# Two gated 3x3 convolutions on one core: the last image's second convolution in four blocks of 7, 7, 7 and 6 slots instead of three of 9, and short first-convolution blocks for one pair of images instead of two

## The reference

```
def qconv_cg(x, w, theta):                 # base = 64 // 4 = 16 channels
    yp = conv3x3(x[:, :base], w[:, :base])
    yr = conv3x3(x[:, base:], w[:, base:])
    d = sigmoid(2.0 * (yp - theta))
    return yp + d * yr

h   = relu(bn(qconv_cg(x, w_a, theta_a)))  # bn: a scale and a shift per channel
h   = bn(qconv_cg(h, w_b, theta_b))
out = relu(x + h)
```

## Time and profile before

| | before |
|---|---|
| median of 3 runs | 434.52 us (434.52 to 435.0) |
| the profiled execution's own time | 434.99 us |
| its span, first to last instruction | 433.1 us |
| time around the span | 1.89 us |
| TensorE (PE) busy | 426.2 us, 98% |
| VectorE (DVE) busy | 246.1 us, 57% |
| ScalarE (ACT) busy | 198.7 us, 46% |
| GpSimd (POOL) busy | 30.8 us, 7% |
| granted TensorE clock, mean | 0.996 |

### The profile page before, as it was taken

One profiled execution on the slowest core, in us unless ns is written; L12 is line 12 of the kernel. 1 busy time (PEld: TensorE's weight loads), 2 busy tenths in 40 slices (PEclk: granted clock), 3 DMA queues, 4 the chain that ended last, 5 costly groups with the idle time before them and its releaser, 6 DMA issues.

```text
span 433.1 us, 17330 instructions
## 1 busy us (share of the span) xinstructions
PE 426.2 (98%) x7823; PEld 423.9 (98%) x7823; DVE 246.1 (57%) x423; ACT 198.7 (46%) x338; POOL 30.8 (7%) x81
## 2 busy tenths in 40 slices
PE   9999999999999999999999999999999999999994
PEld 8999999999999999999999999999999999999993
DVE  6767644753764663574375385366357367436535
ACT  5765444534544553453453453354345355434322
POOL 6041000000000100000000000021000000000001
PEclk9999999999999999999999999999999999999998
DMA  8435116251615110420624161161623321012044
GB/s 166 87 79 98 27 27 123 50 98 29 122 28 101 25 28 4 99 51 2 125 57 82 37 123 29 27 123 25 122 49 62 66 49 39 13 27 49 8 93 94
DMA packets 119802, 27.57 MB, mean 64 GB/s; under 512 B 119408, under 2 KB 119664, under 8 KB 119728
## 3 DMA queue, kind: packets, MB, share of 16 engines
q1 hardware_dynamic: 117760, 26.09, 29.7%
q10 hardware_dynamic: 1648, 0.36, 0.4%
q0 software_dynamic: 320, 0.00, 0.0%
HBM read 13.60 MB, written 12.85 MB: 61 GB/s over the span
## 4 chain that ended last, share of the span: by engine, by line
PE 98%; DVE 1%; issue 0%; ACT 0%; DVEq 0%
PE acc L549 96%; PE acc L500 1%; DVE mix L863 0%; DVE rows_out L911 0%; PE acc L575 0%; PE acc L488 0%; ACT mix L697 0%; PE acc L492 0%; DVE rows_out L953 0%; DVE rows_out L908 0%; ACT rows_out L719 0%; DVEq L862 0%
## 5 line engine op out<-in xcount | busy, mean ns | idle before, releaser
L549 PE MATMUL acc<-x_lo,w_hi 32*128 32x456 f32 (+1 forms) x1392 | 251.3, 358 | 0.0
L549 PE MATMUL acc<-x_hi,w_lo 32*128 32x456 f32 (+1 forms) x1392 | 250.8, 358 | 0.0
L549 PE MATMUL acc<-x_hi,w_hi 32*128 32x456 f32 (+1 forms) x1392 | 250.5, 357 | 0.0
L549 PE MATMUL acc<-h_hi,w_lo 32*128 32x512 f32 x1152 | 244.2, 390 | 0.0
L549 PE MATMUL acc<-h_lo,w_hi 32*128 32x512 f32 x1152 | 243.7, 389 | 0.0
L549 PE MATMUL acc<-h_hi,w_hi 32*128 32x512 f32 x1152 | 243.5, 389 | 0.0
L549 PEld LDWEIGHTS acc<-x_lo,w_hi 32*128 32x128 f32 x1392 | 212.0, 183 | 0.0
L549 PEld LDWEIGHTS acc<-x_hi,w_lo 32*128 32x128 f32 x1392 | 211.8, 183 | 0.1
L549 PEld LDWEIGHTS acc<-x_hi,w_hi 32*128 32x128 f32 x1392 | 211.7, 183 | 0.0
L549 PEld LDWEIGHTS acc<-h_hi,w_hi 32*128 32x128 f32 x1152 | 183.9, 183 | 0.1
L549 PEld LDWEIGHTS acc<-h_hi,w_lo 32*128 32x128 f32 x1152 | 183.4, 183 | 0.0
(11 more groups left out here) (86 smaller groups left out, 161.3 us busy)
## 6 DMA issues: line engine op xcount, KB each, us to landing
out_dram<-rows_out SPq DMA_DIRECT2D x95, 126.0 KB, 2.5
x<-in_x_dram SPq DMA_DIRECT2D x28, 392.0 KB, 5.3
early<-in_x_dram SPq DMA_DIRECT2D x4, 112.0 KB, 3.7
x<-in_x_dram SPq DMA_DIRECT2D x4, 98.0 KB, 3.2
out_dram<-rows_out SPq DMA_DIRECT2D x3, 112.0 KB, 2.4
x<-in_x_dram SPq DMA_DIRECT2D x1, 294.0 KB, 4.3
x<-in_x_dram SPq DMA_DIRECT2D x1, 280.0 KB, 5.0
x<-in_x_dram SPq DMA_DIRECT2D x1, 196.0 KB, 3.5
```

What stands on the lines that cost most here:

```text
L549: return pe.matmul(sums(bank, blk), w[g * ROWS:(g + 1) * ROWS, tap], moving(blk, part, c, dx, g), start=(u == 0 and (alone or g == bank_gr ...
```

## The change

1. `SHORT_PAIRS` goes from 2 to 1: images 2 and 3 are cut like the later ones, into seven blocks of 8 slots instead of eight of 7. There are 57 a blocks.
2. The last image (15) has four b blocks, of 7, 7, 7 and 6 slots (`LAST`), instead of three of 9. They are b45 to b48, and there are 49 b blocks. Six slots are 342 columns.
3. The end of `second` becomes b45, b46, b44, b47, b48, e1 (before: b45, b46, b44, b47, e1).
4. The total stays 108 blocks and 27 rounds, and so does the number of matmuls, 108 x 4 x 18 = 7776.

The order that follows from lines 90 to 97, with the slots of each block, where the two differ most:

| round | before | after |
|---|---|---|
| r0, r1 | a0 to a7, all 7 | the same |
| r2 | a8:7 b0:9 a9:7 b1:9 | a8:8 b0:9 a9:8 b1:9 |
| r3 to r5 | the same pattern, 7 9 7 9 | the same pattern, 8 9 8 9 |
| r6 | a16:8 b8:9 a17:8 b9:9 | a16:8 a17:8 a18:8 a19:8 |
| r7 | a18:8 b10:9 a19:8 b11:9 | b8:9 a20:8 b9:9 a21:8 |
| r8 | a20:8 a21:8 b12:9 a22:8 | b10:9 a22:8 b11:9 a23:8 |
| r9 | b13:9 a23:8 a24:8 a25:8 | b12:9 a24:8 b13:9 a25:8 |
| r24 | b39:9 a56:8 b40:9 a57:8 | a55:8 b40:9 a56:8 b41:9 |
| r25 | b41:9 b42:9 b43:9 b45:9 | b42:9 b43:9 b45:7 b46:7 |
| r26 | b46:9 b44:9 b47:9 e1:8 | b44:9 b47:7 b48:6 e1:8 |

```
-SHORT, SHORT_PAIRS = 7, 2
+SHORT, SHORT_PAIRS = 7, 1
+LAST = (7, 7, 7, 6)
...
-    NB, NE = 3 * B, B // EDGE
+    NE = B // EDGE
...
-        second += [("b", 3 * img + r) for r in range(3)]
+        second += [("b", 3 * img + r) for r in range(3 if img < B - 1 else len(LAST))]
...
-    second[-4:] = [second[-3], second[-2], second[-4], second[-1], ("e", 1)]
+    second[-5:] = second[-4:-2] + [second[-5], second[-2], second[-1], ("e", 1)]

     def b_slots(n):

+        r = n - 3 * (B - 1)
+        if r >= 0:
+            return B - 1, 1 + sum(LAST[:r]), LAST[r]
         return n // 3, 1 + n % 3 * BLK_B, BLK_B
...
-        return BLK_B if kind == "b" else EDGE if kind == "e" else sum(k for img, t, k in a_slots[n])
+        return b_slots(n)[2] if kind == "b" else EDGE if kind == "e" else sum(k for img, t, k in a_slots[n])
```

## The result

The changed kernel takes 436.33 us (median of 8 runs, 435.91 to 438.21) against 434.83 us before (8 runs beside it): 1.0037 times as long, interval 1.0024 to 1.0049. It is slower by about 1.5 us, where 2.25 us were forecast. The profiled execution took 436.14 us, with a span of 434.3 us.

What follows compares the result with a forecast made beforehand. PE, busy 98% of the span with the row groups' matmuls, was taken as the bound. +4.2, -2.15, -0.1 and +0.3 give +2.25 us, 437.2 us from the profile; set on the 434.52 median, 436.8 us, range 435.4 to 438.2.

Steps and rivals of the forecast that it cites:

- Part 1: Everything up to the end of r24: 520 more columns at 8.1 ns each, +4.2 us.
- Part 2: r25 and r26: 512 fewer columns save only 2.15 us instead of 4.2, since nines delay one another.
- the path of nines: r25 and r26: visits through g2, g3, g1, g2, g3 meet nines in all but two pieces; short blocks wait beside it.
- a lead of two matmuls: PE's queue: a row group runs ahead by two matmuls, forgiving 0.46 us at each change of group.
- The sign that I had named: r25 and r26: matmuls of 398 and 342 columns 0.23 us apart beside nines; b44's product at about 425.5 us.
- Part 3: The tail after b44's last visit: chain unchanged, DVE's queue no longer late, 0.1 us less at most; last stores same sizes.
- Part 4: Load of image 7, split a round earlier: PE waits about 0.45 us, +0.3 us in sum, bounds 0 to +1.3.
- Free streams: r25 and r26: no limit on the lead acts there, PE's end moves +0.07 us; 434.6 to 434.9 us, chance 0.10.
- A lead of three: Row groups lead by three matmuls or more: +1.1 to +1.6 us instead of +2.05, 435.7 to 436.4 us; chance 0.17.
- Image 7 late: Image 7's load lands near the slowest 6.8 us or late gates push more: +1 to +1.3 us, 437.5 to 438.1; chance 0.13.

Runs made afterwards that it cites:

- shorts_less2: Changed kernel with two slots of each of the four short blocks b45 to b48 left out (5, 5, 5, 4); 436.2 us.
- b44_less2: Changed kernel with two slots of b44 alone left out (7 instead of 9); 434.32 us.
- cut_777: Kernel before with the last image's three b blocks cut to 7, 7, 7, six slots left out; 432.14 us.
- alternate: Changed kernel with the last image cut 7, 7, 6, 7 and long and short blocks in turn, b44 in r26; 435.6 us, 1.0018 times before.
- img7_late: Changed kernel with the load of image 7 issued behind b9's stores instead of b8's; 440.39 us.

## Why the prediction was right, and where its sizes were off

The direction, the mechanism and the order of the terms held; 1.5 us came instead of 2.25. That the time itself came nearer, 436.33 us against 436.8, is in part luck: the forecast was set on 434.52 us, the median of the first three of the 8 runs of the kernel before, and all 8 give 434.83.

**Part 1 (+4.2 us).** r1 to r24 took 4.05 us more in the first pair of profiles and 4.42 in the second, image 7's 0.1 to 0.2 us included. A small gain may be missing in the term: in the kernel before, where sevens are held in r2, r2 took 15.07 - 14.88 = 0.19 us more than r3 (0.09 in the second profile), and with eights beside nines r2 is no longer than r3. Two profiles of one kernel differ by 0.13 and 0.24 us in r1 to r24, so this is not shown.

**Part 2 (-2.15 us).** Measured -2.27 and -2.29, 0.1 us more than the term. Of all readings in the prediction this one decided the sign: by columns alone it would have been -4.2 and the change a draw. shorts_less2 and b44_less2 show that the path of nines sets the end, and cut_777 (2.0 to 2.2 us saved) and alternate (1.4) fit a lead of two matmuls. That the chip counts exactly two is not shown; it is the whole number that fits these kernels best. The sign that I had named came in part (timeline of the changed kernel, PE, r26): beside b44's nine the six's matmuls are 414.57 - 414.34 = 0.23 us apart and a seven's 415.06 - 414.83 = 0.23, but later, beside the nine in g3, the six's are only 423.83 - 423.67 = 0.16 apart. So the short blocks are not held all the time.

```profile
414.34 0.39 PE L553 MATMUL acc<-h_hi,w_lo 32*128 32x342 f32 x1
414.57 0.39 PE L553 MATMUL acc<-h_hi,w_lo 32*128 32x342 f32 x1
414.83 0.39 PE L553 MATMUL acc<-h_lo,w_hi 32*128 32x398 f32 x1
415.06 0.39 PE L553 MATMUL acc<-h_lo,w_hi 32*128 32x398 f32 x1
...
423.67 0.31 PE L553 MATMUL acc<-h_hi,w_hi 32*128 32x342 f32 x1
423.83 0.32 PE L553 MATMUL acc<-h_hi,w_hi 32*128 32x342 f32 x1
```

**Part 3 (-0.1 us at e1's sum).** b44's product came 1.79 us later than before and the last DVE instruction 430.92 - 429.19 = 1.73 us later: -0.06. POOL's addition ended last, as worked out. The step that failed is its last sentence, that the last stores have the same sizes. e1's store has, but the two blocks ahead of it in the DMA queue are seven and six instead of nine and nine, and the span ends 0.5 us sooner after the last instruction. This is the largest error of a single term.

**Part 4 (+0.3 us).** The place, the wait of some 4 us on ACT and the shift of b10's with_input came as described; the load landed 137.03 - 129.39 = 7.6 us after b8's relu instead of 8.4, so only 0.1 to 0.2 us reached PE, by r8 (15.90 and 16.03 us against 15.82 without the wait). img7_late shows that the cover was used up: a later landing goes straight into the time.

Sum of what the profiles show, first pair: +4.05 in r1 to r24, -2.27 in r25 and r26, -0.04 from the last matmul's start to DVE's end, -0.46 behind it, and -0.02 at the start, gives +1.26 us for the span (434.33 - 433.07). Second pair: +4.42 - 2.29 - 0.04 - 0.49, and +0.31 at the start, gives +1.91 us. Without the start, which does not go with the kernel, the two pairs give +1.28 and +1.60 us. The medians differ by +1.50 us.

**Rivals.** Free streams fell with shorts_less2. A lead of three was given 435.7 to 436.4 us, and the measured 436.33 lies in that too; the time alone does not tell it from the forecast. The two last rounds do: by the prediction's own sum three matmuls save 0.3 + 2.8 = 3.1 us there and two save 2.15, and 2.27 and 2.29 were measured. cut_777 too fits three less well (2.4 us expected, 2.0 to 2.2 measured). Of the sign, b44's product at 425.5 for two and 424.5 for three, 425.12 came, nearer to two. Image 7 late did not come in the changed kernel.

## What to carry to other kernels

When several streams share one issue queue as here, the end is set not by each stream's own work but by the longest path through all of them, less a small lead at every change; so cut the blocks on that path, and check it before shortening anything beside it. Alternating long and short blocks cost little (30.70 us in r25 and r26, where the columns alone would give 34.40 - 4.15 = 30.25), while taking columns from short blocks beside a run of long ones was worth nothing; at the end of a kernel, where nothing gives the lead back, the order of the blocks counts as well as their size (1.4 us here). A load that sits behind stores in a queue is moved by everything that moves the block of those stores: look for the image or tile whose distance shrinks most.

## What the runs showed of the hardware that had not been expected

- A matmul that is held behind other row groups shows it in the trace by its length: the same 284-column matmul is recorded with 0.29 us when free and 0.39 us when held at a nine's pace, and its start distance goes from 0.13 to 0.24 us. (The profile models the ends of matmuls, so the length is a sign in the trace, and the distance is the measured time.)
- Columns that wait cost nothing that these runs can tell: 456 columns less on each row group, 3.7 us by their price, changed the time by less than 0.2 us.
- The end of the span depends on the blocks stored ahead of the last one, down to a floor: from DVE's last instruction it takes 3.9 us with nines, 3.4 us with seven and six, and 3.4 us also with five and four. With nines the DMA engines are 0.98 to 0.99 busy in the last two full microseconds, with five and four only 0.59 to 0.65; that the full queue is the cause was not tested by itself.
